# Two-layer attention and expert kernel: ScalarE in place of SyncE issues the transfers of the score maxima

## What is computed

```python
# x, ctx: (4, 512, 256); 16 heads of 16; everything in float32
x = x + attention0(layernorm(x), ctx, ctx)   # with biases, time bias -0.1*|t - t'|, softmax, output projection
x = x + ffn0(layernorm(x))                   # dense silu FFN, plus 4 heads of product-key top-8 of 1024 experts
x = x + attention1(layernorm(x), ctx, ctx)   # relu projections, softmax
x = x + moe(layernorm(x))                    # top-2 of 8 experts, gelu; the weights come from the normed x
```

## Time and profile before

| what | value |
|---|---|
| median of 3 runs | 1221.88 us (1218.49 to 1224.4) |
| profiled execution, its own time | 1220.31 us |
| its span (first to last instruction) | 1218.5 us |
| busy: PE, PEld | 1063.1 us (87%), 660.5 us (54%) |
| busy: DVE, ACT, POOL | 793.9 us (65%), 642.8 us (53%), 482.7 us (40%) |
| mean granted TensorE clock | 0.93 of full speed |
| transfers of SP's queue (q1), POOL's (q0), ACT's (q10) | 98.67 MB, 47.63 MB, 3.54 MB |

### The profile page before, as it was taken

One profiled execution on the slowest core, in us unless ns is written; L12 is line 12 of the kernel. 1 busy time (PEld: TensorE's weight loads), 2 busy tenths in 40 slices (PEclk: granted clock), 3 DMA queues, 4 the chain that ended last, 5 costly groups with the idle time before them and its releaser, 6 DMA issues.

```text
span 1218.5 us, 16977 instructions
## 1 busy us (share of the span) xinstructions
PE 1063.1 (87%) x5494; PEld 660.5 (54%) x5494; DVE 793.9 (65%) x1991; ACT 642.8 (53%) x858; POOL 482.7 (40%) x508
## 2 busy tenths in 40 slices
PE   8699998989677899998899778999899898799991
PEld 3334343434355777787777554333334334588881
DVE  6666676686488777877877334778777845244443
ACT  2166555566527667767667422565555561255550
POOL 3147886696423244344443331212323333222220
PEclk9699998999979999999999986999998898899996
DMA  7756758566999300000002330465453327222226
GB/s 209 182 180 201 221 178 276 150 215 216 257 237 233 80 1 1 1 1 1 1 1 64 102 78 1 147 173 140 114 166 101 90 65 320 68 71 75 67 66 207
DMA packets 74763, 150.92 MB, mean 124 GB/s; under 512 B 7866, under 2 KB 44620, under 8 KB 73142
## 3 DMA queue, kind: packets, MB, share of 16 engines
q1 hardware_dynamic: 61558, 98.67, 31.1%
q0 software_dynamic: 10800, 47.63, 11.3%
q10 hardware_dynamic: 2320, 3.54, 1.1%
HBM read 73.10 MB, written 76.25 MB: 123 GB/s over the span
## 4 chain that ended last, share of the span: by engine, by line
PE 56%; DVE 24%; ACT 7%; issue 5%; POOL 4%; DMA 3%; SPq 1%; DVEq 0%; POOLq 0%; ACTq 0%
PE ps L1397 13%; PE ps L1305 8%; DVE negmax L1691 7%; PE ps L1272 5%; PE ps L1286 4%; PE ps L1248 4%; PE ps L1257 4%; PE ps L1499 3%; PE ps L1462 3%; PE ps L1476 3%; PE ps L1618 1%; DVE moe_w L2005 1%; PE ps L1314 1%; DVE hl L1696 1%; PE ps L1321 1%
## 5 line engine op out<-in xcount | busy, mean ns | idle before, releaser
L1691 DVE TENSOR_REDUCE negmax<-ps 128x1 f32<-128x512 f32 x512 | 321.8, 682 | 87.0 <-PE ps L1272 86.5
L984 ACT ACTIVATE pt<-ps 128x1024 f32<-128x1024 f32 x256 | 256.3, 1026 | 131.3 <-PE ps L1286 130.6
L1272 PE MATMUL ps<-sk,sq 56*128 56x512 f32 x512 | 163.8, 455 | 39.3 <-DVE negmax L1691 29.4
L1305 PE MATMUL ps<-pt,v_aug 128*32 128x512 f32 x1024 | 145.7, 632 | 1.2 <-POOL pt L726 0.8
L1286 PE MATMUL ps<-sq,sk 57*128 57x512 f32 x512 | 129.8, 495 | 5.9 <-DMA sq<-m_sb 3.7
L1272 PEld LDWEIGHTS ps<-sk,sq 56*128 56x128 f32 x512 | 74.5, 199 | 95.2 <-DVE negmax L1691 78.7
L726 POOL TENSOR_TENSOR pt<-pt,near 128x256 f32<-128x256 f32 x128 | 92.1, 728 | 77.1 <-ACT pt L984 76.6
L1286 PEld LDWEIGHTS ps<-sq,sk 57*128 57x128 f32 x512 | 51.2, 193 | 108.1 <-issue 73.8
L895 POOL DMA_INDIRECT expert_out<-yo,dest x39 | 38.2, 981 | 116.2 <-ACT yo L1172 101.6
L811 POOL TENSOR_TENSOR w_first<-w_first,moe_w 128x1024 f32<-128x1024 f32 x16 | 38.1, 2379 | 107.3 <-DVE pt L1997 106.3
L1462 PE MATMUL ps<-sel,hl 128*128 128x512 f32 x256 | 73.2, 418 | 6.8 <-DVE pt L1997 6.8
(11 more groups left out here) (302 smaller groups left out, 2037.1 us busy)
## 6 DMA issues: line engine op xcount, KB each, us to landing
expert_rows<-zero SPq DMA_DIRECT2D x3, 5586.0 KB, 57.9
expert_weights_split<-wst POOLq DMA_DIRECT2D x8, 2048.0 KB, 8.4
qk_rows<-hl SPq DMA_DIRECT2D x30, 512.0 KB, 5.7
sk<-qk_rows SPq DMA_DIRECT2D x62, 192.0 KB, 4.9
sq<-qk_rows SPq DMA_DIRECT2D x56, 192.0 KB, 4.6
moe_w<-in_w POOLq DMA_DIRECT2D x16, 512.0 KB, 7.0
wexp<-expert_weights_split POOLq DMA_DIRECT2D x16, 512.0 KB, 4.6
wexp<-expert_weights_split SPq DMA_DIRECT2D x4, 2048.0 KB, 17.0
```

What stands on the lines that cost most here:

```text
L984: act.activation(pt[:, 4 * (U % 2) + 2 * half:4 * (U % 2) + 2 * half + 2, :], ps[:, 2 + 2 * half:4 + 2 * half, :], ACT.Exp, scale=(BIAS, S ...
L1272: pe.matmul(ps[:, jbank(job), :], sq[r, pair, t * P:(t + 1) * P], sk[r, pair, :], start=True, stop=True).then_inc(s_job, 1)
L1305: ins = pe.matmul(ps[32 * j:32 * j + 32, OBANK, :], v_aug[:, b % 2, c, HG * g + j, :], pt[:, 4 * (U % 2) + j, :], start=(c == 0), stop=(c ...
L1691: dve.tensor_reduce(negmax[:, n % 2, col:col + 1], src, AX, ALU.max, negate=True).then_inc(s_jd, 1)
```

## The change

`load_max` moves from SP to ACT, with the same wait for DVE's copy (`s_jd`) and the same two transfers. On ACT it runs at the beginning of its step: behind the exponential of half 1 of the step before, ahead of the copies and exponentials of its own. The first one comes at U = -3 of layer 0, ahead of `first_stacks`.

```diff
@@ SP
-            def load_max(L, b, g):
-                n = NG * (B * L + b) + g
-                sp.wait_ge(s_jd, at[L, "m", b, g].done)
-                for s in range(2):
-                    sp.dma_start(sq[HALF * s + MROW:HALF * s + MROW + 1, 2 * g:2 * g + 2, :].bitcast(F32),
-                                 m_sb[8 * s:8 * s + 8, n % 2, :].bitcast(F32)).then_inc(s_mr[n % 2], 16)
...
                 for U in STEPS[L]:
                     for b in range(B):
                         u = U - NU * b
-                        if u + 2 in (0, 4, 8, 12) and (L or U + 2):
-                            load_max(L, b, (u + 2) // 4)
...
             sp.wait_ge(s_ld[1], 64)
-            load_max(0, 0, 0)
@@ ACT
                         for s in range(2):
                             first_query_rows(s)
                     if L == 0 and U == -3:
+                        load_max(0, 0, 0)
+                    for b in range(B):
+                        if U - NU * b + 2 in (0, 4, 8, 12) and (L or U + 2):
+                            load_max(L, b, (U - NU * b + 2) // 4)
+                    if L == 0 and U == -3:
                         for g in range(1, NG):
                             first_stacks(g)
...
+            def load_max(L, b, g):
+                n = NG * (B * L + b) + g
+                act.wait_ge(s_jd, at[L, "m", b, g].done)
+                for s in range(2):
+                    act.dma_start(sq[HALF * s + MROW:HALF * s + MROW + 1, 2 * g:2 * g + 2, :].bitcast(F32),
+                                 m_sb[8 * s:8 * s + 8, n % 2, :].bitcast(F32)).then_inc(s_mr[n % 2], 16)
```

## The result

| | before | after |
|---|---|---|
| median, same chip (8 runs each) | 1221.43 us (1216.26 to 1224.4) | 1231.18 us (1224.06 to 1234.63) |
| profiled execution, its own time | 1220.31 us | 1232.76 us |
| its span | 1218.5 us | 1231.0 us |
| mean granted clock | 0.93 | 0.922 |

The ratio is 1.0083 with an interval of 1.0058 to 1.0108: the change makes the kernel slower, by about 10 us. The forecast was 1219.4 us with a range that ended at 1230, and "same".

What follows compares the result with a forecast made beforehand. PE and DVE were taken to bound the kernel (four fifths of the chain). Terms +2.5 - 5.3 + 1.1 = -1.7 us gave 1218.6 from 1220.31, or 1220.2 from the median; forecast between, 1219.4 us, range 1213.5 to 1230.

Steps and rivals of the forecast that it cites:

- part 3: 30 further groups where ACT waits and issues: mostly covered, +1.1 us together, bounds 0 and +40 us.
- signs of being wrong: New PE idle released by ACT's L984 or POOL's L726, PE still waiting for maxima, start moved under 1 or over 4 us.
- Part 1: Start: first maxima ahead of ACT's stacks delay SP's load of x of batch 2; +2.5 us, bounds 0 and +3.9.
- Part 2: 192 to 208 us: PE's 3.65 us wait for maxima and 1.7 us of low clock vanish; -5.3 us, bounds 0 and -5.3.
- Rival 1: Near 200 us: the stall stays, as another queue doesn't help or it was coincidence; 1224.7 us, chance 0.18.
- plain steps: Steps without extra jobs, 15 of 30: exponentials 1.15 us later, covered by 0.4 us at PE, so cost nothing.
- cover is thinner: Steps U = 2 mod 4: ACT's issues or DVE's late copy delay the second exponential; 16 us more, 1235.4 us, chance 0.13.

Runs made afterwards that it cites:

- stacks_first: The changed kernel with ACT's stacks of groups 1 to 3 issued ahead of the first maxima again; 1222.91 us, ratio 1.0026.
- three_groups_moved: The kernel before with only the maxima of U = 50, 54 and 58 of layer 0 issued by ACT; 1230.07 us, ratio 1.0089.
- start_moved: The kernel before with only the first group (U = -3 of layer 0) on ACT, ahead of its stacks; 1221.5 us, ratio 1.0014.
- zero_held: The changed kernel with SP waiting for layer 0's last maxima ahead of the context loads and zero fill; 1222.74 us, ratio 1.0016.
- both_mended: The changed kernel with ACT's stacks ahead of the first maxima and SP held ahead of context loads and zero fill; 1218.59 us, ratio 1.0000.
- one_group_again: Second run of the kernel before with only the group of U = 30 of layer 0 on ACT; 1215.76 us, ratio 0.9971.
- change_repaired: The changed kernel with five groups of layer 0 (U = -3, 2, 50, 54, 58) back on SP; 1216.72 us, ratio 0.9975.
- before_act_waits: The kernel before, SP issuing all maxima, but ACT waiting for DVE's copy at the head of the 31 steps; 1219.55 us, ratio 1.0023.
- after_again: The changed kernel, unaltered, run and profiled once more against the kernel before; 1232.08 us, ratio 1.0110.

## Why the prediction was wrong

**The step that failed** is the end of part 3: "SP loses 32 waits and 64 issues ... nothing on the chain waits for those." Taking a wait out of a queue is an edit of its own. I asked what the wait's removal does to SP's row writes in the same step, and did not read on to what stands behind the loop: 22 MB of zero fill that start 33 us earlier, while a group of maxima with no slack to spare is still to come. Measured: 3.9 and 4.6 us in the two traces of the change, 1.6 in stacks_first, 6.7 in three_groups_moved, 0 wherever the fill was held, and at most 0.5 where the group went ahead of it. A good part of the size is whether the clock then drops (it did not in stacks_first, where PE's wait was 1.49 us; it did behind 1.73, 2.44 and 3.17 us).

A second step failed, and by as much: the price of the steps in part 3, +1.1 us, where they cost about 6.5 (below). The signs of being wrong that the prediction named were all there: PE idle with ACT's exponential as the releaser (3.0 us in six waits), PE still waiting for the maxima, and group 1 moved by more than 4 us.

**Part 1, the start: +2.5.** The mechanism was right (PE's group 1, ACT's stacks, SP's load of x, DVE's statistics). start_moved gives 2.6, the changed kernel 3.6 and 3.8. Less the 1.9 us that are older than the change, group 1 begins at 46.9 (forecast: 46.3) and x is in at 56.4 (55.2). The term was a little small: ACT's first pair of issues took 1.91 us, not the 1.38 that I took from SP. That is 0.5 of the 1.1 to 1.3 us that the changed kernel's traces lose beyond the forecast; the rest was not traced, and in start_moved it is not there.

**Part 2, the stall: -5.3.** Right: -5.1 and -5.0 between 190 and 210 us, 4.8 to 5.0 in stacks_first, zero_held and both_mended. I had put PE's need 4.8 us behind the issue; counted from the issue's end it came at 5.4 us and the maxima at 5.8, so PE waited 0.42. Rival 1, that the stall stays, fell. That the whole term came back was also luck: with the wait 1 us longer, in one_group_again, the clock fell and 0.9 us was all that came back at this place. The Trainium skill, "DMA: Bandwidth & Descriptors", has two rules on this. By its section "Queues, rings and completion order" each DMA engine takes turns between the queues with work for it; the shorter wait agrees. By "Issuing engines are not separate DMA queues" spreading transfers over issuers saves issue time only; the gain near 200 us speaks against that in this place. The maxima issued into the zero fill took 7.3 us from a queue with nothing else on it, so turns alone keep no short transfer short here.

**Part 3, the steps: +1.1.** Most plain steps cost nothing, as forecast. To see which steps cost something I read the distance from one issue of the maxima to the next. Five steps of layer 0 and one of layer 1 stand out, and they do so in every kernel with that group at the head of ACT's step (but for U = 34 in change_repaired), where kernels with it on SP lose at most 0.5 us at U = 2 and nothing at the others. The step U = 2 of the changed kernel, in its timeline:

```profile
76.36 0.27 DVE L1704 CAST m_sb<-ps 16x128 fp32r<-16x128 f32 x1
...
76.66 1.98 ACTq L990 DMA_DIRECT2D sq<-m_sb  x2
...
78.68 1.04 ACT L970 CAST sel<-wst 128x1024 fp32r<-128x1024 f32 x1 [3.37 <-DVE negmax L1693]
79.63 1.02 ACT L979 ACTIVATE pt<-ps 128x1024 f32<-128x1024 f32 x1
...
80.70 0.50 PE L1288 MATMUL ps<-sq,sk 57*128 57x512 f32 x2 [1.33 <-ACT pt L979]
```

In the kernel before ACT's copy `sel` ran ahead of DVE's copy of the maxima (69.75 against 70.91 us). Now it stands behind the wait and two issues of together 1.98 us, the exponential behind it, and PE waits 1.33 us. The six steps, with the loss in the changed kernel:

- U = 2 (a transpose, and the copy `sel`): 1.6 us, forecast 0.1.
- U = 22 (a transpose): 0.6 us, forecast 0.1.
- U = 34 (a projection, forecast 0): 1.2 us. ACT's pair of issues took 2.48 us, its emptying of the projection came late, DVE's behind it, and `turn_out` waited 1.20 us for DVE. In change_repaired the same pair took 1.29 us, and the step lost nothing (0.03).
- U = 46 (a plain step, forecast 0): 0.9 us, and 0.4 more in the step of U = 50. The pair took 2.05 us, ACT's exponentials began 2.5 us after DVE's copy, POOL's near bias came late and fell behind a long operation of POOL's, and PE's `values` waited for it. change_repaired, with U = 46 on ACT, loses 1.3 us from 262 to 278 us, three_groups_moved, with it on SP, nothing.
- U = 58 (four exponentials in a row): 1.8 us, forecast 0.3. Here PE also waits 1.09 us for the maxima; both_mended, with the fill held, loses 1.7 and waits 1.01. The group of U = 54, a transposing step, costs nothing.
- In layer 1, U = 26 (two transposes): 0.5 us, forecast 0.1.

The rows of U = 34 and of U = 46, both of the kernel after:

```profile
214.66 2.48 ACTq L990 DMA_DIRECT2D sq<-m_sb  x2
...
219.76 0.66 PE L1316 MATMUL ps<-ident,oT 128*128 128x128 f32 x4 [1.20 <-DVE hl L1698]
...
263.38 2.05 ACTq L990 DMA_DIRECT2D sq<-m_sb  x2
...
265.53 3.77 ACT L979 ACTIVATE pt<-ps 128x1024 f32<-128x1024 f32 x4 [3.15 <-DVE negmax L1693]
```

That makes about 6.5 us in layer 0, where the forecast had 1.1. It is the mechanism of the rival "cover is thinner", at under half of its price of 16 us. What failed is the price of a pair, which I took as 1.33 us in every step. The trace of the kernel before already held SP's pairs of U = 10, 22 and 46 at 2.09, 1.94 and 2.06 us; the median of the earlier trace rows hides them:

```profile
260.89 2.06 SPq L517 DMA_DIRECT2D sq<-m_sb  x2
```

ACT's pairs took 2.08, 2.08 and 2.05 us in the same three steps. I had written myself that one issue of 1.39 us would take the cover of a plain step.

**The sum**, from the columns of the changed kernel: 1.9 ahead of the change, 3.6 start, 1.6 the step U = 2, -0.8 to 190 (U = 22 in it, and a place where only the clock differs), -5.1 the stall, 1.3 to 262 (U = 34), 1.4 to 278 (U = 46), 3.9 to 290 (the fill), 1.8 to 332 (U = 58), -1.0 to 691, 3.4 to 740, 0.3 from there on. That is 12.3, against 12.45 between the two executions' own times. The 1.9 are in zero_held, both_mended, change_repaired, three_groups_moved and before_act_waits too, with a lower clock near 37 us, and not in stacks_first or after_again: they belong to the execution.

**Still open** are the 3.4 us between 691 and 740, 3.5 in after_again, and at most 0.3 in any other kernel. In the rows below they are clock alone. The timeline of the kernel before, then of the changed one:

```profile
704.69 0.66 PE L1469 MATMUL ps<-ident,w_first 128*128 128x128 f32 x4 [3.34 <-ACT xn L1030]
...
705.18 1.89 PE L1499 MATMUL ps<-wff 128*128 128x256 f32 x8
```

```profile
713.30 1.12 PE L1471 MATMUL ps<-ident,w_first 128*128 128x128 f32 x4 [3.35 <-ACT xn L1032]
...
714.21 3.62 PE L1501 MATMUL ps<-wff 128*128 128x256 f32 x8
```

The waits are alike, the work is the same; the clock was 1.00 in the one and fell to 0.50 in the other. Nothing that the change touches runs there. Why it fell in both traces of the change was not found; with either of the two repairs it did not. Nor was it tried to cut the transfers' time under the fill, say by a smaller fill.

## What to carry to other kernels

When a waiting instruction leaves an in-order queue, read that queue's program to its end: the wait may be the only thing that keeps a bulk transfer out of a busy stretch, and a line of the timeline (what does SP do once it is free?) shows it. Ask of each moved issue what slack it has: here 27 groups could move and five together could not, and moving a chosen 17 gave 0.5% where moving all lost 0.8%. An issue ahead of a busy engine's own work costs up to its full length (1.3 to 2.5 us for the pair) wherever that work is the next thing asked for; the wait by itself cost nothing. Price a repeated instruction by its longest cases, not by its median: look up each in its own step.

## What the runs showed of the hardware that was not expected

- A pair of issues took 1.28 to 1.40 us on ACT in 26 of the 32 steps and 1.91 to 2.48 us in the other six, with the same bytes and the same code (the same six in after_again, 1.82 to 2.34 us). SP's pairs had three such steps, of 1.94 to 2.09 us, among ACT's six. What they have in common is open. The group of the line in the kernel after (min/median/max of one, in ns), beside the earlier trace rows:

```profile
L990 ACTq DMA_DIRECT2D sq<-m_sb x64: 627/627/1824, 42.6 to 1004.8; - x64
```

- Two transfers of 4 KB, alone on their queue, took 7.1 to 8.0 us from the end of their issue to PE's start while the zero fill ran (278.16 to 285.46 after; 277.42 to 285.08 in three_groups_moved; 8.0 in after_again, 7.1 in stacks_first), and 5.8 us under q and k rows and stacks. The last of their packets ended 5.2 to 5.5 us behind the issue under the fill, 0.7 us with nothing beside them.
- The wait ahead does not by itself decide the granted clock: behind equal waits (3.34 and 3.35 us; 1.36 and 1.36 us) it fell in one kernel and stayed in the other, at a price of 1.7 us for four matmuls in the one case and 3.4 us for the stretch in the other.
